# Score products of the second head attention: one product of 128 stationary columns per batch becomes two of 64 columns

## The reference, cut to what matters

```python
HIDDEN, N_HEADS, HEAD_DIM, N_KV_HEADS = 512, 32, 128, 4
N_GROUPS = N_HEADS // N_KV_HEADS
hidden_states = jnp.concatenate([context, latents], axis=1)      # 64 + 64 = 128 keys
q = (latents @ Wq).reshape(b, q_len, N_KV_HEADS, N_GROUPS, HEAD_DIM)
k = (hidden_states @ Wk).reshape(b, kv_len, N_KV_HEADS, HEAD_DIM)
v = (hidden_states @ Wv).reshape(b, kv_len, N_KV_HEADS, HEAD_DIM)
scores = jnp.einsum('bqhgd,bkhd->bhgqk', q, k) * scale
attn = jax.nn.softmax(scores.astype(jnp.float32), axis=-1).astype(q.dtype)
out = jnp.einsum('bhgqk,bkhd->bqhgd', attn, v)
return out.reshape(b, q_len, N_HEADS * HEAD_DIM) @ Wo
```

## Time and profile before

| | before |
|---|---|
| median of 3 runs | 3335.3 us (3334.0 to 3343.16) |
| the profiled execution | 3344.26 us, its span 3342.5 us |
| PE busy | 3186.6 us, 95% of the span |
| PEld busy | 2537.4 us, 76% |
| DVE, ACT, POOL busy | 1681.9, 1471.4, 1126.6 us |
| granted clock of PE over the span | 0.987 |

### The profile page before, as it was taken

The page is one execution under the profiler, slowest core; times in us unless marked ns, Lnnn a source line. Parts: engine busy times, 40 slices in busy tenths (PEclk is TensorE's granted clock), DMA queues, the critical chain, the costliest instruction groups (busy, mean ns, idle before and its releaser), DMA issues. The chain is left out here.

```text
span 3342.5 us, 55363 instructions
## 1 busy us (share of the span) xinstructions
PE 3186.6 (95%) x21704; PEld 2537.4 (76%) x21708; DVE 1681.9 (50%) x3572; ACT 1471.4 (44%) x3294; POOL 1126.6 (34%) x689
## 2 busy tenths in 40 slices
PE   8888999999999999999999979999999999999997
PEld 5666568888888888888854437888788878888885
DVE  5677444334333433333353566555655565556554
ACT  5666334444444444444322434444444434444443
POOL 6666323232223233322220113334333423334322
PEclk9999999999999999999999989999999999999999
DMA  3000121221212111112012102122111212221201
GB/s 106 2 2 2 42 82 62 65 76 58 70 57 77 63 64 63 64 64 64 20 60 85 38 16 105 64 70 87 58 66 67 77 64 69 65 69 66 74 32 58
DMA packets 56565, 199.92 MB, mean 60 GB/s; under 512 B 8976, under 2 KB 9744, under 8 KB 53008
## 3 DMA queue, kind: packets, MB, share of 16 engines
q1 hardware_dynamic: 56336, 196.76, 17.5%
HBM read 192.54 MB, written 4.19 MB: 59 GB/s over the span
## 5 line engine op out<-in xcount | busy, mean ns | idle before, releaser
L1754 POOL TENSOR_TENSOR h_wol<-h_ro,h_woh 128x1024 fp32r<-128x1024 f32 x128 | 314.5, 2457 | 612.9 <-ACT h_woh L1805 612.9
L1750 POOL TENSOR_TENSOR h_wql<-h_rq,h_wqh 128x1024 fp32r<-128x1024 f32 x128 | 309.0, 2414 | 501.7 <-ACT h_wqh L1800 501.7
L2251 DVE COPY h_tf<-ps 128x512 f32<-128x512 f32 (+1 forms) x256 | 142.5, 557 | 606.7 <-PE ps L2032 606.6
L2255 DVE TENSOR_TENSOR h_ol<-ps,h_oh 128x512 fp32r<-128x512 f32 x256 | 176.7, 690 | 525.8 <-ACT h_oh L1858 525.8
L141 PE MATMUL ps<-h_woh,h_oh 128*128 128x512 f32 x1024 | 428.6, 419 | 5.9 <-DVE h_ol L2255 5.8
L141 PE MATMUL ps<-h_Xh,h_wqh 128*128 128x512 f32 x1024 | 415.5, 406 | 5.2 <-ACT h_sq L1844 1.9
L143 PE MATMUL ps<-h_woh,h_ol 128*128 128x512 f32 x1024 | 406.0, 397 | 0.0
L142 PE MATMUL ps<-h_wol,h_oh 128*128 128x512 f32 x1024 | 405.5, 396 | 0.0
L143 PE MATMUL ps<-h_Xh,h_wql 128*128 128x512 f32 x1024 | 401.8, 392 | 0.0
L142 PE MATMUL ps<-h_Xl,h_wqh 128*128 128x512 f32 x1024 | 400.3, 391 | 0.0
L1908 ACT ACTIVATE h_ex<-ps,h_mx 128x128 f32<-128x128 f32 x512 | 180.9, 366 | 270.9 <-DVE h_mx L2291 270.8
(11 more groups left out here) (298 smaller groups left out, 6302.2 us busy)
## 6 DMA issues: line engine op xcount, KB each, us to landing
h_rq<-in_L_Wq SPq DMA_DIRECT2D x128, 512.0 KB, 3.4
h_ro<-in_L_Wo SPq DMA_DIRECT2D x128, 512.0 KB, 3.4
h_rk<-in_L_Wkv SPq DMA_DIRECT2D x47, 512.0 KB, 3.3
h_craw<-in_ctxT SPq DMA_DIRECT2D x7, 1024.0 KB, 7.3
cnat<-in_ctx SPq DMA_DIRECT2D x4, 1024.0 KB, 8.6
t_craw<-in_ctxT SPq DMA_DIRECT2D x4, 1024.0 KB, 9.4
t_cn<-in_ctx SPq DMA_DIRECT2D x4, 1024.0 KB, 5.5
out_rows<-x SPq DMA_DIRECT2D x16, 256.0 KB, 2.5
```

Source lines behind the costliest of these rows:

```text
L1750: nc.gpsimd.tensor_tensor(wql[:, par], rq[:, par], f(wqh[:, par]), ALU.subtract).then_inc(m["p_wq"], 1)
L1754: nc.gpsimd.tensor_tensor(wol[:, par], ro[:, par], f(woh[:, par]), ALU.subtract).then_inc(m["p_wo"], 1)
L2251: nc.vector.tensor_copy(tf[:], ps[:, TBK, 0:PT]).then_inc(m["v_t"], 1)
L2255: nc.vector.tensor_tensor(by_head(ol), ps[:, AB, :].rearrange("p (b h t) -> p b h t", h=2, t=S), f(by_head(oh)), ALU.subtract).then_inc(m[ ...
```

## The change

The branch on `norm` in `scores` is removed, and both attentions take the form with two products.

```diff
                             for b4 in range(HB):
                                 b = HB * (t % 2) + b4
-                                if norm:
-                                    for h in range(2):
-                                        last = nc.tensor.matmul(ps[S * h:S * h + S, SBK, b4 * KEYS:(b4 + 1) * KEYS],
-                                                                qf[:, pair, b, h], kf[:, b], start=True, stop=True)
-                                else:
-                                    last = nc.tensor.matmul(ps[:, SBK, b4 * KEYS:(b4 + 1) * KEYS],
-                                                            qf[:, pair, b].rearrange("p h t -> p (h t)"), kf[:, b],
-                                                            start=True, stop=True)
+                                for h in range(2):
+                                    last = nc.tensor.matmul(ps[S * h:S * h + S, SBK, b4 * KEYS:(b4 + 1) * KEYS],
+                                                            qf[:, pair, b, h], kf[:, b], start=True, stop=True)
                             last.then_inc(m["s_s"], 1)
```

## The result

| | before | after |
|---|---|---|
| median | 3338.1 us (4 runs) | 3377.5 us (4 runs, 3373.2 to 3381.5) |
| ratio | | 1.0118, 95% interval 1.0102 to 1.0135 |
| the profiled execution | 3344.3 us | 3373.7 us |

The change costs 39 us (34 to 45), against a forecast of 3379 and +43. A fourth run of the kernel before had moved its median from 3335.3 to 3338.1.

The account below looks back on a forecast made before the run. PE's chain of products was taken to bound L1: steady difference zero, edges 0.35 us x 128 steps = +44.8 us, less 1.4 for waits, so +43.4 on the median 3335.3, rounded 3379 us; range 3366 to 3392.

Parts of the forecast that it names:

- What bounds L1: L1's attention: a chain of PE products with nothing between, so added PE time reaches the end, less 1.4 us.
- Way in: From L2040 to the first L1 score record: the array is emptied first, +0.10 us a step, as in L3.
- First pair and way out: From the first L1 score record to L142: uncovered first load and leaving the halved array, +0.25 us a step.
- Steady part: L1's score records within a step: 8 pairs cost what 8 records did, 0.112 us each, difference zero.
- Clock: L1's granted clock might fall from 1.00 to L3's 0.99, costing up to 12 us more.
- Rival 2: Only one edge of L1's halved scores is paid: way in +13 us, the rest alone +32; chance 0.04.
- rival 3: L1's edges are hidden and only the steady part counts: no difference, within 10 us; chance 0.05.
- The factor of up to 2 for 64 stationary columns: Skill's rule for array packing: L1's 16 score records cost as much as 8, sum 3335.3 us; beside rival 3.
- Rival 4: L1's 64-column weight loads are not covered: 0.054 us a pair, +100 us with the edges, 3435 us; chance 0.03.
- The rule beside it: Loads overlap matmuls in flight only when row groups differ, so every L1 score pair would pay its load.
- Rival 5: L1's halves do not run side by side with 128 moving columns: +160 us with edges, 3495 us; chance 0.02.
- Rival 6: L1's pair interval is set by the 64-column load, 0.058 us: -10 us with edges, 3325 us; chance 0.02.

Follow-up runs that it names:

- the order of eight and eight: Against the changed kernel: L1's halved score products ordered as eight for one head, then eight for the other; 3437.0 us.
- the first two experiments: Against the kernel before, L1 scores in halves for only the second batch of four: 3380.4 us; for only the first and third batches: 3421.4 us.
- the third: Against the changed kernel: L1's `values_of`, right ahead of the scores, made in halves too; 3376.4 us.
- four and four: Against the changed kernel: L1's halved score products ordered as four for one head, then four for the other, per two batches; 3381.2 us, ratio to before 1.0138.

## Why the prediction was right

- **What bounds L1.** PE's order does, alone. The added time of a step came out at the end in full, less 0.7 us of waits (1.4 were taken off).
- **Way in.** Forecast +0.10 us, measured +0.09.
- **First pair and way out.** Forecast +0.25, measured +0.24. The first pair took 0.17 to the second, as forecast. Carrying both over from L3's 64 moving columns to L1's 128 was right.
- **Steady part.** I took 0.112 us a pair, and the straight line between L3 and L418 had given 0.110; by the first to last record it is 0.11. Eight times 0.002 is 0.016 us of the step. The sum of the step is 0.33, not 0.35, and 127 x 0.33 = 42 (so many ways in and out lie between the first and the last scores) less 0.7 us of waits is 41, against the 40.2 of L1. The term that was mis-sized is this one, by 2 us in all; the rest of the overshoot is rounding of the rows.
- **The number.** The change costs 39 us where 43 were forecast. That the median lies only 1.5 us from 3379 is in part luck: the forecast stood on a median before of 3335.3, and the fourth run moved it up by 2.8.
- **Clock.** The 12 us held ready for a lower clock in L1 were not needed: L1 is granted 1.00 after as before. The drops lie elsewhere, and differ between executions.
- **The rivals.** Rival 2 (one edge) and rival 3 (no difference) are out by the timeline. The factor of up to 2 for 64 stationary columns, which the Trainium skill gives (TensorEngine Tiling (Array Packing), Theoretical Speedup), agrees with the steady part, where two records in halves take the 0.11 us of one; the edges come on top. Rival 4 is out by the 0.11 of a pair; it wants 0.112 + 0.054 = 0.17. The rule beside it, from the Trainium skill (TensorE: Matmul & The Clock Gate, Part 3, "What overlaps and what doesn't"), that a load overlaps only with another row group's matmuls, is not what this trace shows: all records use 128 rows, and sixteen loads of 0.137 us each span only 0.85 us, under the matmuls. Rival 5 is out by the same 0.11, and the order of eight and eight shows what it looks like when the halves do not alternate. Rival 6 is out: a pair follows its moving columns, 0.058 us for 64 and 0.11 for 128.

That the edges are the cause is shown by the first two experiments and the third: the cost stays with a quarter of the halved products, doubles with two excursions (a way in and a way out each), and does not rise when twice the products are halved within one excursion. How the 0.33 us of an excursion divide between the emptying of the array and uncovered loads was read from the timelines, not tested by a run.

## What to carry to other kernels

Splitting a product over the halves of the array paid in this kernel only where the whole one is held by its weight load (128 stationary and 64 moving fp32 columns), and not with 128 and 128; other types were not measured. Count the places where PE changes between whole and halved products, not the products: here a way in and a way out cost 0.33 us together. Put halved products next to each other and let the order alternate between the halves. An edge that falls into a wait of PE cost nothing here (15 ways in with the values in halves), and one removed where PE waits anyhow gives little back.

## What was not expected of the hardware

- Halves overlap beyond direct neighbours. With eight records for one half and then eight for the other, about four of each overlapped (1.58 us where one by one would be about 1.97 and side by side is 1.09), the second eight starting with the fifth record of the first. With four and four nearly all did (1.14).
- An fp32 record of 128 stationary columns takes 0.11 us with 64 moving columns as with 128, and its weight loads start every 0.11 us in both.
